# Two stage boundaries of a gated cross-attention program: value stores ahead of the second keys, third operands at once, and the banded attention's first batch loaded one stage early

## What is computed

```python
x = x + tanh(g_xattn[0]) * L0_xattn(layernorm(x), ctx)   # 64 heads of 16, softmax over 128 keys
x = x + tanh(g_ffn[0])   * L0_ffn(layernorm(x))          # one 1024x1024 weight plus 16 low-rank updates
x = x + tanh(g_xattn[1]) * L1_xattn(layernorm(x), ctx)   # 1x1 convolutions over tokens, attention in a band of 16
x = x + tanh(g_ffn[1])   * L1_ffn(layernorm(x))          # 1024x1024, masked by clusters that the tokens hit
```

## Time and profile before

| | |
|---|---|
| median of 3 runs | 2052.22 us (2049.05 to 2054.82) |
| the profiled execution's own time | 2051.24 us |
| its span | 2049.1 us |
| PE busy | 1948.1 us, 95% of the span |
| VectorE, ScalarE, GpSimd busy | 1072.4, 681.4, 360.1 us |
| DMA | 328.62 MB, mean 160 GB/s |

### The profile page before, as it was taken

How to read it: one execution, slowest core, us unless ns; L and a number is a source line. 1 busy time by engine, 2 the same in 40 slices (tenths; PEclk the granted TensorE clock), 3 DMA queues, 4 the chain that set the end, 5 groups by cost and what they waited for, 6 DMA issues and landing times. The chain is left out here.

```text
span 2049.1 us, 50169 instructions
## 1 busy us (share of the span) xinstructions
PE 1948.1 (95%) x20126; PEld 1582.2 (77%) x20126; DVE 1072.4 (52%) x1868; ACT 681.4 (33%) x1152; POOL 360.1 (18%) x332
## 2 busy tenths in 40 slices
PE   7999889999997999999999899999689999999999
PEld 7999889999996777777777477777467777777887
DVE  5444241112114555555555465555578888874445
ACT  2222231111102344444434211111156666665121
POOL 0000000000001111111101210000256666651000
PEclk9999999999997899999999999999799999999999
DMA  5332335433348545544543434544664444433434
GB/s 200 124 123 103 145 106 184 169 122 137 116 163 300 204 167 215 203 174 190 226 185 115 161 113 185 184 184 164 198 188 149 140 131 142 148 113 114 150 134 147
DMA packets 149431, 328.62 MB, mean 160 GB/s; under 512 B 56433, under 2 KB 82673, under 8 KB 141105
## 3 DMA queue, kind: packets, MB, share of 16 engines
q1 hardware_dynamic: 147344, 326.04, 44.5%
q10 hardware_dynamic: 1952, 0.60, 0.1%
HBM read 200.25 MB, written 125.83 MB: 159 GB/s over the span
## 5 line engine op out<-in xcount | busy, mean ns | idle before, releaser
L1191 ACT ACTIVATE a_pt<-a_st_bank 128x1024 f32<-128x1024 f32 x128 | 131.3, 1026 | 266.3 <-PE a_st_bank L1239 266.3
L1528 POOL TENSOR_TENSOR a_sm<-a_sm,a_nmax 113x1024 f32<-113x1024 f32 x84 | 159.7, 1908 | 89.2 <-DVE a_nmax L1581 89.2
L1137 DVE TENSOR_REDUCE a_nmax<-a_s_bank 128x8 f32<-128x1024 f32 x124 | 151.7, 1223 | 20.6 <-PE a_s_bank L1227 14.0
L226 PE MATMUL q_qb<-q_xt_hi,wq_hi 128*128 128x256 f32 x512 | 146.2, 286 | 2.8 <-DVE wq_lo L168 2.8
L226 PE MATMUL kv_banks<-kv_ct_hi,wk_hi 128*128 128x256 f32 x512 | 146.0, 285 | 2.9 <-DVE wk_lo L168 2.9
L226 PE MATMUL kv_banks<-kv_ct_hi,wk_lo 128*128 128x256 f32 x512 | 145.5, 284 | 0.0
L226 PE MATMUL q_qb<-q_xt_lo,wq_hi 128*128 128x256 f32 x512 | 145.4, 284 | 0.0
L226 PE MATMUL q_qb<-q_xt_hi,wq_lo 128*128 128x256 f32 x512 | 145.4, 284 | 0.0
L226 PE MATMUL kv_banks<-kv_ct_lo,wk_hi 128*128 128x256 f32 x512 | 145.4, 284 | 0.0
L1821 PE MATMUL a_s_bank<-a_ks,a_qs 64*49 64x256 f32 x1344 | 95.5, 399 | 24.4 <-DMA a_ks<-k 11.8
L1575 DVE TENSOR_TENSOR a_sm<-a_s_bank,a_band 113x1024 f32<-113x1024 f32 x84 | 102.6, 1222 | 21.4 <-PE a_s_bank L1821 18.2
(11 more groups left out here) (228 smaller groups left out, 4595.2 us busy)
## 6 DMA issues: line engine op xcount, KB each, us to landing
k<-raw SPq DMA_DIRECT2D x32, 512.0 KB, 4.6
a_qs<-q SPq DMA_DIRECT2D x16, 1024.0 KB, 5.2
a_ks<-k SPq DMA_DIRECT2D x16, 1024.0 KB, 7.1
a_vraw<-v SPq DMA_DIRECT2D x32, 304.0 KB
q_xin<-in_x SPq DMA_DIRECT2D x16, 512.0 KB, 5.6
q<-q_out_lo SPq DMA_DIRECT2D x16, 512.0 KB, 4.1
q<-q_out_hi SPq DMA_DIRECT2D x16, 512.0 KB, 4.8
kv_cin<-in_ctxT SPq DMA_DIRECT2D x8, 1024.0 KB, 5.5
```

The lines of the kernel that those rows point to most:

```text
L226: m = pe.matmul(out, a(x, c), b(y, c), start=(i + j == 0), stop=(len(terms) * j + i == n - 1))
L1137: dve.tensor_reduce(to, scores[:].rearrange("p b (h x) -> p b h x", h=4), X, ALU.max, negate=True).then_inc(maxed, 1)
L1191: act.activation(pt[:, s % 2], st_bank[:].rearrange("p b (h x) -> p (b h) x", h=4), ACT.Exp).then_inc(expd, 1)
L1528: pool.tensor_tensor(sm[live, k], sm[live, k], nmax[live, k, :].unsqueeze(2).to_broadcast([LIVE, 16, KEYS]), ALU.add).then_inc(shifted, 1)
```

## The change

It changes five things, all at the two boundaries.

1. `last_keys` and `unit_keys` go away. SP issues the last value stores as soon as the values are there. The keys of slot 1 have an ordinary tile of `attention0`, and `load_half` loads them in the filling of that stage (unit 4), on the semaphore `first_in[1]`.
2. The wait before slot 2's load (unit 8) goes away; a wait for `rowed` 1 (ScalarE has written the first row of maxima) stands before slot 3's load (unit 12). The wait for the last value stores moves from step -12 to -5, with one for the key stores.
3. Slot 0 of `ks` and `qs` and the band get places at SBUF address 0 that `ffn0_project1` keeps free (`HOLD`, partly under the low-rank factors). POOL zeroes them there after the last low-rank `product`.
4. SP loads batch 0's `q1`, `k1` and the band in the last turn of `ffn0_project1`, in step 1, ahead of that step's `load_ctx`; six DMAs on one semaphore, `op_in`.
5. In the last stage the two memsets of slot 0, the wait `pads[0]` and those six DMAs are gone. `f1_hi` is split into two tiles that take the freed places.

```diff
@@ project_kv @@
-        e.q_first, e.k_first = [q0, q1], [k0, k1]
+        e.q_first, e.k_first = [q0, q1], [k0]
...
                     unit_queries(0)
-                    unit_keys(0)
+                    sp.dma_start(e.k_first[0][:].rearrange("p s t -> p (s t)").bitcast(F32),
+                                 e.k0[0][:, :, 0:16 * P].rearrange("r j x -> (r j) x")).then_inc(e.first_in[0], 16)
                     sp.wait_ge(clo, done(G - 1))
                     unit_queries(1)
-            def last_keys(s):
-                if s == 1:
-                    sp.wait_ge(k_out, 160 * G + START)
-                    unit_keys(1)
...
-            staggered(sp, G, 2, [(2, load), (None, first_units), (None, output_weights), (0, store_k), (None, last_keys), (0, store_v)],
+            staggered(sp, G, 2, [(2, load), (None, first_units), (None, output_weights), (0, store_k), (0, store_v)],
@@ ffn0_project1 @@
+        sb("f0_hold", [P, HOLD - 4 * D])
+        e.op_zero = later(e, nc, "a_op_zero"); e.op_in = later(e, nc, "a_op_in")
...
+            def first_operands(s):
+                if s == 1:
+                    sp.wait_ge(e.op_zero, 2)
+                    for j in range(2):
+                        sp.wait_ge(qk_out[j][0], 16 + START)
+                    sp.dma_start(e.qs_first[:, 0:D], e.q1[0]).then_inc(e.op_in, 16)
+                    for c in range(4):
+                        sp.dma_start(e.ks_first[c:P:4, c, PADL:PADL + D], e.k1[0][c:P:4, :]).then_inc(e.op_in, 16)
+                    sp.dma_start(e.band[:], e.i["band"]).then_inc(e.op_in, 16)
+
-            steps = [(4, load_x), (1, load_ctx), (0, store_qk(1, e.k1)), (1, store_x2),
+            steps = [(None, first_operands), (4, load_x), (1, load_ctx), (0, store_qk(1, e.k1)), (1, store_x2),
...
+            pool.wait_ge(w.lr, NC)
+            pool.memset(e.ks_first[:], 0.0).then_inc(e.op_zero, 1)
+            pool.memset(e.qs_first[:, D:DPAD], 0.0).then_inc(e.op_zero, 1)
@@ attention0 @@
-        ks = e.k_first + [sb(f"a0_ks{k}", [P, pairs, P], F32R) for k in range(2, 4)]
+        ks = e.k_first + [sb(f"a0_ks{k}", [P, pairs, P], F32R) for k in range(1, 4)]
...
+            sp.wait_ge(e.k_out, 160 * (B // 2 - 1) + START)
...
-                if s % G or filling(u):
+                if s % G or filling(u) and u == 0:
                     return
                 slot, b = s // G, 2 * i + s // NU
-                if isinstance(u, int) and u == NU:
-                    sp.wait_ge(shift_in[0], 16)
+                if isinstance(u, int) and u == NU + G:
+                    sp.wait_ge(rowed, 1)
                 sp.wait_ge(st_done, done(u - 13))
                 part = slice(slot % 2 * pairs * P, (slot % 2 + 1) * pairs * P)
-                sp.dma_start(qs[slot][:].rearrange("p s t -> p (s t)").bitcast(F32),
-                             rows_twice(e.q0[b][:, :, part])).then_inc(qk_in[slot], 16)
+                came = e.first_in[1] if filling(u) else qk_in[slot]
+                if not filling(u):
+                    sp.dma_start(qs[slot][:].rearrange("p s t -> p (s t)").bitcast(F32),
+                                 rows_twice(e.q0[b][:, :, part])).then_inc(came, 16)
                 sp.dma_start(ks[slot][:].rearrange("p s t -> p (s t)").bitcast(F32),
-                             e.k0[b][:, :, part].rearrange("r j x -> (r j) x")).then_inc(qk_in[slot], 16)
+                             e.k0[b][:, :, part].rearrange("r j x -> (r j) x")).then_inc(came, 16)
...
-                if s == -12:
+                if s == -5:
                     for k in range(2):
                         sp.wait_ge(e.v_out[k], 16 * (B // 2) + START)
+                    sp.wait_ge(e.k_out, 160 * (B // 2) + START)
@@ attend1_select_ffn1 @@
-            sp.wait_ge(pads[0], 2)
...
+                    if isinstance(t, int) and t == 0:
+                        continue
...
-                if s == -16:
-                    sp.dma_start(band[:], e.i["band"]).then_inc(const, 16)
...
-            pool.memset(ks[:, 0, 2:4], 0.0).then_inc(pads[0], 1)
-            pool.memset(qs[:, :, D:DPAD], 0.0).then_inc(pads[3], 1)
+            pool.memset(qs1[:, D:DPAD], 0.0).then_inc(pads[3], 1)
...
-            dve.memset(ks[:, 0, 0:2], 0.0).then_inc(pads[0], 1)
...
-            dve.memset(ks[:, 1], 0.0).then_inc(pads[1], 1)
+            dve.memset(ks1[:], 0.0).then_inc(pads[1], 1)
...
-            dve.wait_ge(const, 16)
+            dve.wait_ge(e.op_in, 96)
...
-                    if first(g) == s:
-                        pe.wait_ge(qk_in[g % 2], 80 * (2 * i + g // 2 + 1))
+                    if first(g) == s and LOOP * i + g == 0:
+                        pe.wait_ge(e.op_in, 96)
+                    elif first(g) == s:
+                        pe.wait_ge(qk_in[g % 2], 80 * (2 * i + g // 2 + g % 2))
@@ program @@
+            e.ks_first, e.qs_first, e.band = placed(nc, 0, ("a_ks0", [P, 4, DPAD], F32), ("a_qs0", [P, DPAD], F32),
+                                                    ("a_band", [P, KEYS], F32))
```

More of the change, by code:

```diff
@@ L46 @@
 DPAD = 1048
+HOLD = 5312
 NCL = 64
@@ L550, in unit_queries @@
                              rows_twice(e.q0[0][:, :, part])).then_inc(e.first_in[slot], 16)
-            def unit_keys(slot):
-                part = slice(16 * P * slot, 16 * P * (slot + 1))
-                sp.dma_start(e.k_first[slot][:].rearrange("p s t -> p (s t)").bitcast(F32),
-                             e.k0[0][:, :, part].rearrange("r j x -> (r j) x")).then_inc(e.first_in[slot], 16)
             def first_units(s):
@@ L1340, in attend1_select_ffn1 @@
         x_bank = ps("se_x_bank", [P, 2, 512])
-        const = sem("a_const"); zeroed = sem("a_zeroed"); pads = [sem(f"a_pads{k}") for k in range(4)]; ps_zeroed = sem("a_ps_zeroed"); go = sem("a_go")
+        zeroed = sem("a_zeroed"); pads = [sem(f"a_pads{k}") for k in range(4)]; ps_zeroed = sem("a_ps_zeroed"); go = sem("a_go")
         qk_in = [sem(f"a_qk_in{k}") for k in range(2)]
@@ L1892, in chunk @@
             def chunk(t, s, h, c):
-                for x, w in ((f1_hi_t, f1_hi), (f1_hi_t, f1_lo), (f1_lo_t, f1_hi)):
-                    m = pe.matmul(s_bank[:, h, :], x[s % 2][:, c, :], w[:, c, h * 512:(h + 1) * 512],
-                                  start=c == 0 and w is f1_hi and x is f1_hi_t, stop=c == NC - 1 and x is f1_lo_t)
+                for n, (x, w) in enumerate(((f1_hi_t, f1_hi(c)), (f1_hi_t, f1_lo[:, c, :]), (f1_lo_t, f1_hi(c)))):
+                    m = pe.matmul(s_bank[:, h, :], x[s % 2][:, c, :], w[:, h * 512:(h + 1) * 512],
+                                  start=c == 0 and n == 0, stop=c == NC - 1 and n == 2)
                 if c == NC - 1:
```

31 lines of the change are left out of this document (18 added, 13 removed).

## The result

**Slower by 0.2%.** The changed kernel took 2054.35 us (median of 20 runs, 2050.03 to 2059.06), the kernel before 2050.82 us beside it (20 runs, 2039.98 to 2055.15): ratio 1.002, 95% interval 1.001 to 1.0029, that is +4.1 us, 2.1 to 5.9 (the two medians differ by 3.5). The forecast was 2046.4, with a range up to 2052.0. The last boundary gave what was forecast and a little more. Three other places took 2.7 to 4.1 us each in this execution, one of them where no line of the prediction looks.

The account below looks back on a forecast made before the run. PE is busy for 95% of the span, so only its standstills at the two boundaries can give anything. 2051.24 - 3.85 (last boundary) - 0.95 (first boundary) = 2046.4 us, chance 0.40; range from 2041.5 to 2052.

Parts of the forecast that it names:

- Last boundary: Start of the last stage: first `mask` starts at about 1467.1 instead of 1470.95, bound by VectorE's remaining memset; gain 3.85 us.
- The two "issue" waits: PE's waits of 3.3 and 1.9 us, 40 us after the last boundary's wait, without a nameable cause; left as they are.
- I set at nothing, with its cover: Third GEMM: POOL's 3.8 us of memsets fit 7.4 us of room, and SP's six DMAs leave the context 7 us early.
- First boundary: Start of `attention0`: unit 8 starts at 661.5 instead of 662.44, a gain of 0.95 us.
- 0.45 us for its packets: First boundary: the shift copy's packets take 0.45 us once the queue has drained, so `score_t` begins at 657.1, 2.5 us later.
- The stage's earlier begin, 2.65 us: First boundary: value stores go out earlier, so the new stage begins 2.65 us earlier, with PE at 643.1.
- at 650.4, unit 4 starts 0.3 us earlier than before: First boundary: slot 1's keys, now third load of the stage, land between 648.7 and 652.9, taken as 650.4; wait some 2.3 us.
- So a shift copy waits for what SP issued before it: First boundary: the copy, issued at 652.2 behind 5.24 MB on SP's queue, waits until 656.3.
- fourth units' loads overtake the copy: First boundary rival, chance 0.12: slot 3's 2.1 MB get ahead, unit 8 starts 4.1 to 7.1 us later; 2051.5 to 2054.5.
- Clock: After both boundaries: PE's rise from 1.2 to 2.4 GHz may fall a step earlier or later, up to 2 us either side.
- the two fast rivals: Shift copy not held up at the first boundary (0.18): 2043.6; clock or "issue" waits in favour (0.15): 2041.2 to 2044.4.
- a part gets lost later: Rival, chance 0.15: the last boundary's 3.85 us reaches the end only in part, through clock or "issue" waits; 2048 to 2050.

Follow-up runs that it names:

- e10: The changed kernel with POOL's `ks_first` memset in four pieces of 1048 elements instead of one of 4192; 2052.3 us, ratio 1.0015 to the kernel before.
- e3: The changed kernel with POOL's two memsets ahead of the third `pow` in the third GEMM instead of behind it; 2050.49 us, ratio 1.0008 to the kernel before.
- e1: The changed kernel with slot 3's loads held until the first shift copy has landed, instead of for `rowed` 1 alone; 2054.07 us, ratio 1.0021 to the kernel before.
- e4: The changed kernel with both the edits of e1 and e3: slot 3 held, POOL's memsets early; 2048.35 us, ratio 0.9983 to the kernel before.
- e5: e4 with the second half of `f1_hi` and the odd `f_xt_hi` moved by 128 bytes; 2047.36 us, ratio 0.9978 to the kernel before.
- e8: e5 with the first layer's `a0_att`, `wo_xt_hi` and `wo_xt_lo` also 128 bytes higher; 2046.3 us, ratio 0.9974 to the kernel before.
- e6: The kernel before with `f1_hi` alone, in one piece, 128 bytes higher; 2052.41 us, ratio 1.0012 to the kernel before.
- e7: The kernel before with every tile of the last stage 128 bytes higher; run once, 2050.03 us.
- p1: The kernel before with only the change's first boundary; 2052.53 us, ratio 1.0005 to the kernel before.
- e9: e5 with slot 1's keys, slot 2's operands and first values loaded first, bias and the rest after the shift copy; 2043.57 us, ratio 0.9973 to the kernel before.

## Why the prediction was wrong

**Last boundary: right.** Forecast 3.85 us, measured 4.23 or 4.24 in nine of the ten traces that have it (3.60 in e10, where `mask` starts 6.02 us after the release as well). Its reasoning, that the 11.8 us are not the gain and the remaining memset binds, is what the rows show. The two "issue" waits stayed, 3.0 and 2.3 us (3.3 and 1.9 before).

**Third GEMM: the step "I set at nothing, with its cover" failed**, by 2.84 us. The cover was checked for POOL only: 7.4 us of room for 3.8 us of work, and POOL indeed is late for nobody: its next `pow` waits 6.15 us for VectorE. What was not asked is which operation of another engine runs in those 3.8 us. The memset began 0.09 us before the very `tensor_scalar` that the `pow` ahead of it had released, and that is no accident, since both hang on the same `pow`. The rule is in the Trainium skill ("SBUF — State Buffer", section "Who interferes with whom"): a `tensor_scalar` or copy of VectorE in a two-port mode and GpSimd exclude each other for the whole instruction, and the one issued first wins. The trace agrees, with 0.81 us against 4.12, and e3 and e10 show it by experiment. SP's six DMAs were hidden, as forecast (they carry 1.05 MB and 32 KB, not 1.03 MB): from 1250 to 1450 us the two traces differ by 0.00.

**First boundary: forecast -0.95 us, measured +0.3 to +4.1.** The step that failed most is the shift copy's "0.45 us for its packets", which took 4.7. Three terms:
- The stage's earlier begin, 2.65 us: measured 2.77 (6.11 less 3.34).
- Slot 1's keys "at 650.4, unit 4 starts 0.3 us earlier than before", with a wait of some 2.3 us. The wait was 4.58, since the load came 7.9 us after its issue; unit 4 starts 8.8 us after PE's first score of the stage and not 7.3. From 641 to 646 SP's queue starts only 41 to 184 KB in each half microsecond, while 416 GB/s would be 208; on the forecast's scale unit 4's keys came near 651.9, closer to its slow end (652.9) than to its fast one (648.7).
- "So a shift copy waits for what SP issued before it", until 656.3: its packets began at 655.55 in a trace that runs 2.07 us ahead of the one before, so 1.3 us later than forecast, because unit 4 was; from issue to first packet 4.03 us went by, forecast 4.1. This was right. But once begun, it had to share with what SP issued *after* it: its 34 packets were spread over 4.7 us, where the forecast had 0.45. So `score_t` came 8.2 us later than before and not 2.5, and unit 8 4.65 later and not 0.95 earlier; this is the rival "fourth units' loads overtake the copy", given 0.12, whose condition (ScalarE issues first, so the copy is ahead) came true and did not protect. The Trainium skill ("DMA: Bandwidth & Descriptors", section "Queues, rings and completion order") has the DMA engines take turns between the queues, a packet at a time. For the start of the copy the trace does not agree (4.03 us, and 3.9 to 4.1 in e1, e4, e5 and e8 too); once the copy had begun it does, with 34 packets among 311. With slot 3 held the boundary costs -0.1 us in the mean of four traces (-1.65 to +1.01), so even without that rival the gain of 0.95 us is not shown, nor is it excluded.

**Last GEMM: no step at all**, +2.74 us. The section on the change tells that `f1_hi` is split and moved, and the prediction has no term for it: a tile's address was taken for something without a price. e5, e6 and e7 show that it has one.

**Clock: no loss from it is seen.** The granted clock was at its lower level for 37.5 us at the first boundary (34.1 before) and for 20.5 us at the last (23.9 before). At the first, the difference does not grow after unit 8: 4.65 us there, 4.07 at 700. The last 3 us before each of these four rises hold no idle time of PE.

The chances followed from this. The forecast's 0.40 and the two fast rivals' 0.33 had no loss in them at all; the overtaking (0.12) and "a part gets lost later" (0.15) had one each. In the changed kernel's trace the overtaking's 4.07 us and the last boundary's 4.23 cancel, and two further losses, 2.84 and 2.74 us, present in every trace that has their cause, made the sign. The measured 2054.35 us lies within the 2051.5 to 2054.5 that the overtaking rival gave, but that is luck: the rival had neither of these two.

## What to carry to other kernels

When work is put into an engine's idle time, look at what *other* engines run in that very stretch: a GpSimd instruction started by the same event as a VectorE `tensor_scalar` or copy holds it up for its whole length, and moving it by one statement gives this back. When tiles of a GEMM that runs without a gap are moved, compare the mean time of its matmuls to the nanosecond; in such a GEMM here it paid to keep the start addresses of moving and stationary operands at the same remainder by 256, in another product (e8) it did not. When a small copy must pass a queue full of large loads, hold back what comes after it too, because being issued first by 0.1 us did not protect it here.

## What was not expected of the hardware

- TensorE slows by 1 to 2% in a gapless GEMM when, of its moving rows and its weights, some start at a multiple of 256 bytes and some 128 past one: 226.7 ns per matmul with all at 128 (before, e5) and with all at 0 (e7), 228.9 with `f_hi` alone at 0 (e6), 230.8 with two tiles at 0 (changed). The slow pattern of 96 intervals repeats to 1 ns in each turn of the loop and in all six kernels with the changed placement. The Trainium skill ("SBUF — State Buffer", section "Who interferes with whom") calls TensorE's two read ports, for the moving operand and for the weights, independent, and says that it never waits on anyone; the runs show a dependence. Whether the two reads disturb each other or something else does, no run here shows, and the output product (e8) doesn't follow the rule.
- One and the same order of issues gave 3.53, 5.7, 7.3 and 7.43 us of waiting for a copy of 16 KB. In three of the four its first packet ran 3.9 to 4.0 us after the issue (3.1 in p1); the last one followed within 0.5 us where the wait was 3.53, and 3.8 to 4.7 us later in the others.
- At the start of a stage DMAs move slowly: 41 to 184 KB start in a half microsecond from 641 to 646 in the changed kernel, 180 to 238 from 646.5 to 652. The bias load, which repeats one row to all partitions and comes first there, is not the cause by itself. In e9, where it is issued late and alone, it lands 3.2 us after its issue with up to 0.19 MB in a half microsecond (from 655.0), and e9's own first microseconds, with slot 1's keys in the bias's place, have the dip too (0.09 MB from 642.0 and from 643.0). In both, the last value stores are still under way in a part of that time; what makes the dip no run shows.
- From 1250 to 1450 us, PE's operations of any two traces keep their distance to 0.01 us, so a difference of 1 us in such a place can be read from single profiles, while the times of whole runs spread by 7 to 18 us.
